# A four-stage image kernel: two PSUM banks for du*B with the products in front of the scans, transposes in one bank, and h in a ring of three

## The chip, the cores and the metric

One core of a Trainium2 chip. The metric is the device time of the kernel in microseconds, median over runs. The core has five engines that run their own in-order queues: TensorE (PE, matmuls, with weight loads shown as PEld), VectorE (DVE), ScalarE (ACT), GpSimd (POOL) and SyncE (SP, which issues most transfers). PSUM has eight banks of 128 partitions x 512 fp32 numbers.

## The reference

The input x is 32 images of 128 channels x 32 x 32, fp32. Four layers follow one another:

1. Quaternion batch normalisation. Channels form 32 groups of four; the covariance over batch and pixels is factored (Cholesky), and the input is whitened, mixed by a 4x4 weight per group and shifted. Once the statistics are known, this is one 128x128 matrix `m0` and a column of constants.
2. A Mamba block on each image as a sequence of L = 1024 pixels. With inner width 256 (two halves h of 128) and 16 states:

```
xn = layernorm(x);  xi, z = split(xn @ W_in.T)
xc = silu(causal_conv4(xi));  dt, B, C = split(xc @ W_x.T)
delta = softplus(dt @ W_dt.T + b_dt);  A = -exp(A_log)
h_t = h_{t-1} * exp(delta_t * A) + (delta_t * xc_t) * B_t      # 16 states for each inner channel
y_t = sum over states of h_t * C_t
out = ((y + xc * Dp) * silu(z)) @ W_out.T + x
```

3. Self-attention on the 1024 pixels of each image (one head, width 128), times gamma, plus its input.
4. A non-local block: again softmax attention on the 1024 pixels (theta, phi, a value projection), then batch normalisation over the whole batch, plus the input.

## The kernel before, in words

After the statistics of layer 1 (about the first 150 us) the kernel goes over the 32 images; the loops are unrolled, so every engine has its full list of instructions in a fixed order, and counting semaphores (`wait(engine, name, image, count)`) tie the lists together. The main function of each engine is `image(b, scan, more, att, late)`: while image b is in the scan, the attention stages of image b-1 and the tail of image b-2 run beside it, and the front part (layer norm to delta) of the next half image too. A batch normalisation over the stored results ends the kernel.

An image has two half images (chunks c = 0, 1 of 512 pixels) of 16 steps r = 0 to 15 each. A step k = 16 c + r serves one half h of the inner channels (r < 8 or r >= 8) and two of the 16 states (j = 0, 1). What a step does:

- ACT, `decay`: da = exp(delta * A) for the next step, two instructions (line 680), into a ring of two.
- DVE, `scans(b, k, j)`: `psD` = B row x du (line 484; du lies in PSUM as `psU`, copied there at r = 0 and r = 8, line 477) and the recurrence as one `tensor_tensor_scan` from da and psD into `hs` (line 488). For j = 0 and then j = 1. psD is one bank, so a product waits for the scan before it. hs is a ring of two (`sl = k % 2`).
- POOL, `products`: C rows x hs for both states (line 300), their sum (306), on odd steps the sum of two steps (310), and at r = 14, 15 delta and du for the next half image (286, 291).
- PE, `sum_states` ("add" in the order below): on odd steps adds POOL's result into psY by an identity matmul.
- DVE, `gate`: y * silu(z) from psY.

Attention works on 16 tiles of 128 queries for each image, eight for each half image, at steps `TILE_AT` = 7, 8, 10, 11, 13, 14, 16, 17 (16 and 17 are r = 0 and 1 of the next half image). Tile t goes: PE `energy` (1024 columns into the two banks of psE) -> DVE `row_max`, nm, at the end of the step (line 513) -> ACT `numer`, p = exp(E - max) (line 726) -> PE `turn`, eight transposes of p at steps `TURN_AT` = 8, 10, 12, 12, 14, 15, 17, 18, four into each bank of psT (line 987), -> ACT `turned_out`, two copies of psT into pt (line 690) -> PE `values` ("weigh0", "weigh1"), p times values for two tiles into psA -> ACT `spread`, rb (line 736) -> DVE `attended` (lines 528, 531, 535, 538). Energies of the next tile wait for p of this one, since psE is one pair of banks. `project` makes queries (psE) and keys (psT), `project_values` the values (psT).

The front part uses the same banks: centre, variance, inner0, gates and steps write psT, inner1 and rows psA. ACT reads them in `front(fb, fc, r)` at the steps AT_C = 0 and 1, AT_X = 5 and 7, AT_Z = 9, AT_B = 10, AT_P = 11 (and softplus's Exp and Ln at 13 and 14); it loads a table of functions for Silu and one to go back.

PSUM before: psE 2 banks, psT 2, psY, psU, psD, psA one each: all eight. PE's work within a step is a written list, `ORDER`. ACT's order within a step: key, front (r = 5), decay of the next step, spread, query, value, front (others), residual, turned_out, front (r = 9), numer.

## Time and profile before

| what | value |
| --- | --- |
| runs | 5652.95, 5642.84, 5648.49 us; median 5648.49 |
| profiled execution | 5654.98 us, its span 5653.2 us |
| mean granted TensorE clock | 0.955 |
| busy: PE | 4649.7 us (82%) |
| busy: DVE | 5067.2 us (90%) |
| busy: ACT | 3709.2 us (66%) |
| busy: POOL | 4724.3 us (84%) |
| DMA | 1216.87 MB, 215 GB/s |

The busy times are sums over the whole span; the statistics in front and the batch normalisation at the end use PE, DVE and POOL little, so the shares in the middle are higher. "PE busy" counts matmuls whose ends are modelled. A timeline row gives an instruction's start and duration, and neighbours on one engine can overlap by some hundredths of a microsecond; start-to-start distances are what adds up. Matmuls of fp32 are recorded as two instructions each.

### The profile page before, as it was taken

How to read it: one execution, taken by the hardware profiler on the slowest of the kernel's cores; microseconds unless marked ns; L12 is line 12 of the kernel's file. 1: busy time of each engine (PE TensorE's matmuls, PEld its weight loads, DVE VectorE, ACT ScalarE, POOL GpSimd, SP SyncE). 2: the span in 40 equal slices, each digit the busy share in tenths (PEclk: the TensorE clock that was granted, in tenths of full speed). 3: DMA queues.
4: the chain of work that ended last, by engine and by line, in shares of the span. 5: the costliest groups of instructions: out<-in, count | busy, mean ns of one | idle time of the engine just before them, and what ended most of it. 6: DMA issues, size and time to landing. Idle time of an engine off the chain costs nothing.

```text
span 5653.2 us, 61917 instructions
## 1 busy us (share of the span) xinstructions
PE 4649.7 (82%) x17331; PEld 2705.2 (48%) x17331; DVE 5067.2 (90%) x5978; ACT 3709.2 (66%) x6077; POOL 4724.3 (84%) x3342
## 2 busy tenths in 40 slices
PE   6568888888888888888888888888888888888871
PEld 6135554455445444545444455445445544554450
DVE  4699999999999999999999999999999999999933
ACT  3456677667766766676677667766666776677633
POOL 0698999999989889898989998989889899999910
PEclk9689999999999999999999999999999999999995
DMA  4456656655655565555556665665566566656517
GB/s 132 176 224 224 224 208 223 229 222 216 224 224 215 215 225 217 216 219 225 223 207 224 224 225 217 222 220 212 219 224 223 210 221 229 224 208 224 219 74 301
DMA packets 199100, 1216.87 MB, mean 215 GB/s; under 512 B 27881, under 2 KB 28657, under 8 KB 67697
## 3 DMA queue, kind: packets, MB, share of 16 engines
q1 hardware_dynamic: 194416, 1196.26, 57.4%
q10 hardware_dynamic: 4352, 16.78, 0.7%
q8 instruction: 136, 2.23, 0.2%
q14 instruction: 196, 1.60, 0.1%
HBM read 1158.43 MB, written 54.53 MB: 215 GB/s over the span
## 4 chain that ended last, share of the span: by engine, by line
PE 38%; DVE 22%; ACT 14%; issue 13%; POOL 10%; DMA 1%; DVEq 0%; SPq 0%; POOLq 0%; ACTq 0%
PE psA L814 13%; PE psE L814 11%; DVE hs L488 8%; DVE psD L484 7%; PE psT L814 7%; POOL pa L300 5%; PE psT L987 4%; ACT da L680 4%; ACT p L726 3%; DVE nm L513 3%; PE psY L814 2%; POOL pa L306 2%; POOL pa L310 1%; ACT L649 1%; ACT pt L690 1%
## 5 line engine op out<-in xcount | busy, mean ns | idle before, releaser
L300 POOL TENSOR_TENSOR pa<-hs,rows_all 128x1024 f32<-128x1024 f32 x1024 | 2412.8, 2356 | 396.8 <-DVE hs L488 396.5
L680 ACT ACTIVATE da<-delta,neg_a 128x512 f32<-128x512 f32 x2048 | 1382.1, 719 | 288.3 <-DVE hs L488 276.2
L484 DVE TENSOR_TENSOR psD<-rows_all,psU 128x512 f32<-128x512 f32 x2048 | 1416.5, 692 | 84.7 <-POOL hlast L304 6.3
L306 POOL TENSOR_TENSOR pa<-pa 128x512 f32<-128x512 f32 x1024 | 1317.1, 1286 | 40.2
L488 DVE TENSOR_TENSOR_SCAN hs<-da,hlast,psD 128x512 f32<-128x512 f32 x1024 | 1310.9, 1280 | 36.3
L488 DVE TENSOR_TENSOR_SCAN hs<-da,psD 128x512 f32<-128x512 f32 x1024 | 1249.4, 1220 | 35.2
L814 PE MATMUL psA<-pt,va 128*128 128x256 f32 x4096 | 989.5, 391 | 71.2 <-DVE x L531 43.7
L814 PEld LDWEIGHTS psA<-pt,va 128*128 128x128 f32 x4096 | 770.0, 194 | 295.5 <-DVE x L531 77.1
L513 DVE TENSOR_REDUCE nm<-psE 128x1 f32<-128x1024 f32 x512 | 620.1, 1211 | 201.1 <-PE psE L814 198.8
L726 ACT ACTIVATE p<-psE,nm 128x1024 f32<-128x1024 f32 x512 | 571.5, 1116 | 316.8 <-DVE nm L513 316.7
L690 ACT ACTIVATE pt<-psT 128x512 f32<-128x512 f32 x1024 | 555.5, 596 | 304.4 <-PE psT L987 301.0
L310 POOL TENSOR_TENSOR pa<-pa 128x512 f32<-128x512 f32 x512 | 651.1, 1272 | 40.1
L814 PE MATMUL psY<-pa,ident 128*128 128x512 f32 x1024 | 547.3, 617 | 156.0 <-POOL pa L310 153.5
L987 PE MATMUL psT<-ident,p 128*128 128x128 f32 x4096 | 546.6, 277 | 128.6 <-ACT p L726 128.6
L814 PE MATMUL psE<-ka,x 128*128 128x512 f32 x1024 | 530.8, 644 | 122.2 <-ACT p L726 122.2
L987 PEld LDWEIGHTS psT<-ident,p 128*128 128x128 f32 x4096 | 472.4, 143 | 317.3 <-issue 167.5
L814 PE MATMUL psE<-ka,qa 128*128 128x512 f32 x1024 | 505.5, 617 | 71.4 <-ACT p L726 71.4
L814 PEld LDWEIGHTS psE<-ka,x 128*128 128x128 f32 x1024 | 196.8, 201 | 371.9 <-issue 188.7
L814 PEld LDWEIGHTS psE<-ka,qa 128*128 128x128 f32 x1024 | 194.1, 195 | 330.1 <-issue 195.1
L814 PEld LDWEIGHTS psY<-pa,ident 128*128 128x128 f32 x1024 | 178.8, 194 | 350.8 <-issue 225.9
L286 POOL TENSOR_TENSOR delta<-delta,sp_l 128x512 f32<-128x512 f32 x128 | 163.1, 1274 | 179.8 <-ACT sp_l L671 179.8
L814 PE MATMUL psT<-xn,w_conv 128*128 128x512 f32 x512 | 235.2, 602 | 4.6 <-DVE xn L468 4.5
(186 smaller groups left out, 5017.6 us busy)
## 6 DMA issues: line engine op xcount, KB each, us to landing
rows_all<-bc_scratch SPq DMA_DIRECT2D x1024, 1024.0 KB, 4.7
xin<-x SPq DMA_DIRECT2D x40, 512.0 KB, 7.7
xres<-x SPq DMA_DIRECT2D x64, 256.0 KB, 6.1
x_scratch<-x SPq DMA_DIRECT2D x32, 512.0 KB, 4.3
f_scratch<-fa SPq DMA_DIRECT2D x32, 512.0 KB, 6.8
xres<-x SPq DMA_DIRECT2D x8, 512.0 KB, 3.6
x1g<-x SPq DMA_DIRECT2D x8, 512.0 KB, 3.7
fa<-x SPq DMA_DIRECT2D x8, 512.0 KB, 3.7
```

The costliest lines, as they stand in the source:

```text
L286: pool.tensor_tensor(delta[:, h, cols(fc)], delta[:, h, cols(fc)], sp_l[:, h, :], ALU.add).then_inc(S["delta_ok"], 1)
L300: pool.tensor_tensor(pa[:, k % PROD, :, :], hs[:, sl, :, :], rows_all[:, slot, 2:4, :], ALU.mult).then_inc(S["prod"], 1)
L306: pool.tensor_tensor(pa[:, k % PROD, 0, :], pa[:, k % PROD, 0, :], pa[:, k % PROD, 1, :], ALU.add).then_inc(S["pair"], 1)
L310: pool.tensor_tensor(pa[:, k % PROD, 0, :], pa[:, (k - 1) % PROD, 0, :], pa[:, k % PROD, 0, :], ALU.add).then_inc(S["quad"], 1)
L484: dve.tensor_tensor(psD[:, :], rows_all[:, slot, j, :], psU[:, :], ALU.mult).then_inc(S["dbu_ok"], 1)
L488: dve.tensor_tensor_scan(hs[:, sl, j, :], da[:, sl, j, :], psD[:, :], hlast[:, h, n_:n_ + 1] if ch else 0.0, ALU.mult, ALU.add).then_inc(S ...
L513: dve.tensor_reduce(nm[:, i % 2:i % 2 + 1], flat(psE), AX, ALU.max, negate=True).then_inc(S["nm_ok"], 1)
L680: act.activation(da[:, k % 2, j, :], delta[:, h, cols(ch)], ACT.Exp, scale=neg_a[:, h, 2 * q + j:2 * q + j + 1]).then_inc(S["da_ok"], 1)
L690: act.activation(pt[:, i // GT % 2, 4 * q:4 * q + 4, 128 * (t % GT):128 * (t % GT) + 128], psT[:, q, :].rearrange("p (j i) -> p j i", j=4) ...
L726: act.activation(p[:, i % 2, :], flat(psE), ACT.Exp, bias=nm[:, i % 2:i % 2 + 1], accum_out=rsum[:, i % (2 * GT):i % (2 * GT) + 1]).then_i ...
L814: return pe.matmul(dst, lhsT, rhs, start=start, stop=stop)
L987: last = pe.transpose(psT[:, q, 128 * j:128 * j + 128], p[:, i % 2, (4 * q + j) * 128:(4 * q + j + 1) * 128], ident[:, :])
```

## The change

- `psD` gets two banks, one for each j. `psA` loses its own bank and becomes the second bank of psT (`psA = psT[:, 1, :]`). Statistics' leftovers in psA and psD move accordingly.
- DVE: `scans` is split in `inputs` (the psU copy, now between the two scans of the last step of the group before), `spread_inputs` (both products, in front) and `scan_state`. The layer-norm product of r = 3 stands between products and scans.
- `hs` is a ring of three, indexed over images; da stays a ring of two.
- Transposes of a tile all go through psT's first bank, in two halves `turn0`, `turn1` (for the second tile of r = 12: `more0`, `more1`), each half waiting for ACT's copy of the one before it.
- Keys go through psE: `project` is split in `project_queries` (r = 5) and `project_keys` (r = 6, waits for the queries' copy); ACT's `key` moves behind decay and query. inner1 goes before keys and values, and its copy on ACT is at r = 6 (before: 7), in front of decay.
- gates and steps are split by half: gates1 at r = 8, gates0 at r = 9; steps0 at r = 11, steps1 at r = 12, both steps through the first bank, ACT's Abs and Relu at r = 11 and 12. The variance goes to the first bank.
- `residual` is split: its input matmul (`residual_input`, "resx") stands between the halves of a transpose.

```diff
@@
-        psD = ps("psD", [128, CH])
+        psD = ps("psD", [128, 2, CH])
         psT = ps("psT", [128, 2, CH])
-        psA = ps("psA", [128, CH])
+        psA = psT[:, 1, :]
...
-        AT_C, AT_N, AT_X, AT_Z, AT_B, AT_P = 0, 3, (5, 7), 9, 10, 11
+        AT_C, AT_N, AT_X, AT_Z, AT_B, AT_P = 0, 3, (5, 6), 9, 10, 11
...
-                    sl, slot = k % 2, k % RING
+                    sl, slot = (b * STEPS + k) % HRING, k % RING
...
+                def inputs(b, k):
+                    ch, h = divmod(k // PAIRS, NH)
+                    wait(dve, "du_ok", b, k // PAIRS + 1)
+                    wait(dve, "dbu_ok", b, 2 * k)
+                    dve.tensor_copy(psU[:, :], du[:, h, cols(ch)]).then_inc(S["u_ok"], 1)
+
+                def spread_inputs(b, k):
+                    slot = k % RING
+                    if k % PAIRS == 0:
+                        wait(dve, "u_ok", b, k // PAIRS + 1)
+                    at(dve, f"rl{slot}", (b * (STEPS // RING) + k // RING + 1) * 16)
+                    for j in range(2):
+                        wait(dve, "h_ok", b, 2 * (k - 1) + j + 1)
+                        dve.tensor_tensor(psD[:, j, :], rows_all[:, slot, j, :], psU[:, :], ALU.mult
+                                          ).then_inc(S["dbu_ok"], 1)
+
+                def scan_state(b, k, j):
...
+                    sl = (b * STEPS + k) % HRING
                     if j == 0:
-                        at(dve, f"rl{slot}", (b * (STEPS // RING) + k // RING + 1) * 16)
-                        wait(dve, "prod", b, k - 1)
-                        wait(dve, "hlast_ok", b, min(k - 1, NS))
-                    wait(dve, "h_ok", b, 2 * k + j)
-                    dve.tensor_tensor(psD[:, :], rows_all[:, slot, j, :], psU[:, :], ALU.mult).then_inc(S["dbu_ok"], 1)
+                        wait(dve, "prod", b, k - HRING + 1)
+                        wait(dve, "hlast_ok", b, min(k - HRING + 1, NS))
                     wait(dve, "dbu_ok", b, 2 * k + j + 1)
                     wait(dve, "da_ok", b, 2 * k + j + 1)
                     n_ = 2 * q + j
-                    dve.tensor_tensor_scan(hs[:, sl, j, :], da[:, sl, j, :], psD[:, :],
+                    dve.tensor_tensor_scan(hs[:, sl, j, :], da[:, k % 2, j, :], psD[:, j, :],
                                            hlast[:, h, n_:n_ + 1] if ch else 0.0, ALU.mult, ALU.add
                                            ).then_inc(S["h_ok"], 1)
...
                             if scan:
-                                scans(b, k, 0)
+                                spread_inputs(b, k)
                             if front_of and r == AT_N:
                                 normed(*front_of)
+                            if scan:
+                                scan_state(b, k, 0)
+                            if scan and k % PAIRS == PAIRS - 1 and (k < STEPS - 1 or more):
+                                inputs(*((b, k + 1) if k < STEPS - 1 else (b + 1, 0)))
...
                             if scan:
-                                scans(b, k, 1)
+                                scan_state(b, k, 1)
...
-                def turn(a, m, t, front):
+                def turn(a, m, t, q, front):
                     i = TILES * m + t
-                    wait(pe, "p_ok", a, i + 1)
...
-                    for q in range(2):
-                        wait(pe, "pt_ok", a, 2 * (i - 1) + q + 1)
-                        for j in range(4):
-                            last = pe.transpose(psT[:, q, 128 * j:128 * j + 128],
-                                                p[:, i % 2, (4 * q + j) * 128:(4 * q + j + 1) * 128], ident[:, :])
-                        last.then_inc(S["turn"], 1)
+                    if q == 0:
+                        wait(pe, "p_ok", a, i + 1)
...
+                    wait(pe, "pt_ok", a, 2 * i + q)
+                    for j in range(4):
+                        last = pe.transpose(psT[:, 0, 128 * j:128 * j + 128],
+                                            p[:, i % 2, (4 * q + j) * 128:(4 * q + j + 1) * 128], ident[:, :])
+                    last.then_inc(S["turn"], 1)
...
+                def project_keys(a, m, scan):
                     if m == 0:
...
+                        wait(pe, "q_ok", a, 1)
                     else:
                         wait(pe, "out_ok", a, NG // 2)
+                        if scan:
+                            wait(pe, "x1g_ok", a + 1, 1)
+                    for c in range(NCH):
+                        last = mm(psE[:, c, :], (w_k_t, tp_t)[m][:, :], (x1, x2)[m][:, cols(c)])
+                    last.then_inc(S["k_mm"], 1)
...
                 ORDER = [
                     "centre add variance",
-                    "add energy turn weigh0",
-                    "weigh1 turn add residual",
+                    "add energy turn0 weigh0 turn1",
+                    "weigh1 turn0 resx turn1 residual",
                     "weigh0 weigh1 add",
                     "inner0 add",
-                    "project add",
-                    "project_values add inner1",
+                    "query inner1 add",
+                    "key values",
                     "energy add",
-                    "skip0 energy turn add",
-                    "gates add energy_next",
-                    "rows turn add",
-                    "add energy steps weigh0",
-                    "turn weigh1 turn_more skip1 add energy_next",
+                    "skip0 energy turn0 gates1 turn1",
+                    "gates0 add energy_next",
+                    "rows turn0 turn1",
+                    "add energy steps0 weigh0",
+                    "steps1 weigh1 turn0 skip1 turn1 more0 energy_next more1",
                     "add",
-                    "weigh0 energy turn add",
-                    "turn weigh1 add energy_next",
+                    "weigh0 energy turn0 turn1",
+                    "turn0 weigh1 turn1 add energy_next",
                 ]
```

## Rows read from the trace of the kernel before

**Rows 1.** Busy us of PE, PEld, DVE, ACT, POOL in 2000:3000; clock, DMA share, GB/s

```profile
2000.00:3000.00 1000.00, 858.47 (x3140) 493.11 (x3138) 943.89 (x1089) 693.81 (x1145) 902.38 (x638) 0.98 0.60 220
```

**Rows 2.** Waits, whole span: who, for whom: us, times, longest

```profile
POOL pa L300 <- DVE hs L488: 396.5, 480, 2.6
...
DVE nm L513 <- PE psE L814: 198.8, 149, 7.0
...
DVE psD L484 <- POOL hlast L304: 6.3, 5, 2.1
```

**Rows 3.** Timeline of DVE, plain steps: start us, duration us, instruction

```profile
2726.06 1.28 DVE L488 TENSOR_TENSOR_SCAN hs<-da,hlast,psD 128x512 f32<-128x512 f32 x1
2727.38 0.70 DVE L484 TENSOR_TENSOR psD<-rows_all,psU 128x512 f32<-128x512 f32 x1
2728.11 1.28 DVE L488 TENSOR_TENSOR_SCAN hs<-da,hlast,psD 128x512 f32<-128x512 f32 x1
2729.53 0.70 DVE L484 TENSOR_TENSOR psD<-rows_all,psU 128x512 f32<-128x512 f32 x1
```

**Rows 4.** Timeline of DVE, scan before a row maximum

```profile
2701.32 1.28 DVE L488 TENSOR_TENSOR_SCAN hs<-da,hlast,psD 128x512 f32<-128x512 f32 x1
2702.51 1.20 DVE L513 TENSOR_REDUCE nm<-psE 128x1 f32<-128x1024 f32 x1
```

**Rows 5.** Timeline of DVE, gate before a product

```profile
2711.54 0.67 DVE L494 TENSOR_TENSOR du<-psY,sz 128x512 f32<-128x512 f32 x1
2712.13 0.69 DVE L484 TENSOR_TENSOR psD<-rows_all,psU 128x512 f32<-128x512 f32 x1
```

**Rows 6.** Page, part 5, transposes' copies: busy us, mean ns | idle before, releaser

```profile
L690 ACT ACTIVATE pt<-psT 128x512 f32<-128x512 f32 x1024 | 555.5, 596 | 304.4 <-PE psT L987 301.0
```

**Rows 7.** Timeline, row maxima of r = 7, 8, 11, 13, 14, 0 and what lies between

```profile
2737.69 1.20 DVE L513 TENSOR_REDUCE nm<-psE 128x1 f32<-128x1024 f32 x1
...
2743.50 1.20 DVE L513 TENSOR_REDUCE nm<-psE 128x1 f32<-128x1024 f32 x1
...
2744.73 1.11 ACT L726 ACTIVATE p<-psE,nm 128x1024 f32<-128x1024 f32 x1 [1.01 <-DVE nm L513]
...
2753.81 1.06 ACT L690 ACTIVATE pt<-psT 128x512 f32<-128x512 f32 x2
...
2759.70 1.23 DVE L513 TENSOR_REDUCE nm<-psE 128x1 f32<-128x1024 f32 x1 [1.25 <-PE psE L814]
...
2767.01 1.08 ACT L690 ACTIVATE pt<-psT 128x512 f32<-128x512 f32 x2 [0.55 <-PE psT L987]
...
2770.03 1.22 DVE L513 TENSOR_REDUCE nm<-psE 128x1 f32<-128x1024 f32 x1 [0.95 <-PE psE L814]
2770.14 0.63 ACT L671 ACTIVATE sp_l<-sp_e 128x512 f32<-128x512 f32 x1
...
2771.29 1.11 ACT L726 ACTIVATE p<-psE,nm 128x1024 f32<-128x1024 f32 x1 [0.51 <-DVE nm L513]
...
2775.92 1.20 DVE L513 TENSOR_REDUCE nm<-psE 128x1 f32<-128x1024 f32 x1
...
2785.56 1.20 DVE L513 TENSOR_REDUCE nm<-psE 128x1 f32<-128x1024 f32 x1
```

**Rows 8.** Chain of waits, r = 1 to 7 of another half image: start, us

```profile
2628.09 0.87 PE psT L987 x8
...
2640.21 0.86 PE psY L814 x2
...
2647.98 1.12 ACT ka L698
...
2654.64 1.73 PE psE L814 x4
```

**Rows 9.** Busy time by engine from p at r = 8 to p at r = 10

```profile
2744.73:2755.97 11.24, 7.64 (x23) 2.87 (x21) 10.89 (x13) 11.18 (x18) 9.64 (x6) 1.00 0.51 187
```

More of the change, by code:

```diff
@@ L381, in _ @@
                 dve.wait_ge(S["st_centred"], NB)
[L382 removed]
+                link(dve.tensor_copy(gram[:, :], psD[:, 0, 0:128]))
                 for j in range(4):
@@ L757, in image @@
                                 query(b - 1)
+                            if att and r == 6:
+                                key(b - 1, c)
                             if att and r == 7:
                                 value(b - 1, c)
-                            if front_of and r not in (AT_X[0], AT_Z):
+                            if front_of and r not in (*AT_X, AT_Z):
                                 front(*front_of, r)
@@ L846, in st_gram @@
                         blk = turned[q][:, 128 * j:128 * j + 128]
-                        last = mm(psD[:, 0:128], blk, blk, start=start and j == 0, stop=stop and j == 3)
+                        last = mm(psD[:, 0, 0:128], blk, blk, start=start and j == 0, stop=stop and j == 3)
                     last.then_inc(S["st_gram"], 1)
@@ L887, in front @@
                         mm(psT[:, 0, :], m0c[:, :], xin[:, cols(fc)]).then_inc(S["cent_mm"], 1)
-                    if what == "gates":
-                        if att:
-                            wait(pe, "pt_ok", *att["turned0"])
-                        else:
-                            wait(pe, "xi_ok", fb, 2 * fc + 2)
-                        for h in range(NH):
-                            mm(psT[:, h, :], w_in_t[:, DI + C * h:DI + C * h + C],
-                               xn[:, KC - 1 + fc * CH:KC - 1 + fc * CH + CH]).then_inc(S["z_mm"], 1)
@@ L896, in front @@
-                    if what == "steps":
-                        wait(pe, "rows_ok", fb, fc + 1)
-                        wait(pe, "z_ok", fb, 2 * fc + 2)
-                        if att:
-                            wait(pe, "pt_ok", *att["turned1"])
-                        for h in range(NH):
-                            mm(psT[:, h, :], w_dt_t[BCR:BCR + DR, C * h:C * h + C], rows_out[BCR:BCR + DR, :]
-                               ).then_inc(S["dpre_mm"], 1)
+                    if what in ("gates1", "gates0"):
+                        h = int(what == "gates1")
+                        wait(pe, "xi_ok", fb, 2 * fc + 2)
+                        if att and h == 1:
+                            wait(pe, "v_ok", *att["valued"])
+                        if att and h == 0:
+                            wait(pe, "pt_ok", *att["turned0"])
+                        mm(psT[:, h, :], w_in_t[:, DI + C * h:DI + C * h + C],
+                           xn[:, KC - 1 + fc * CH:KC - 1 + fc * CH + CH]).then_inc(S["z_mm"], 1)
@@ new lines, in front @@
+                    if what in ("steps0", "steps1"):
+                        h = int(what == "steps1")
+                        if h == 0:
+                            wait(pe, "rows_ok", fb, fc + 1)
+                            wait(pe, "z_ok", fb, 2 * fc + 2)
+                            if att:
+                                wait(pe, "pt_ok", *att["turned1"])
+                        else:
+                            wait(pe, "sp_abs", fb, 2 * fc + 1)
+                            wait(pe, "sp_relu", fb, 2 * fc + 1)
+                        mm(psT[:, 0, :], w_dt_t[BCR:BCR + DR, C * h:C * h + C], rows_out[BCR:BCR + DR, :]
+                           ).then_inc(S["dpre_mm"], 1)
@@ L955, in residual, with energy @@
                     last.then_inc(S["x1_mm"], 1)
-                def energy(a, m, t, scan):
+                def energy(a, m, t):
                     i = TILES * m + t
@@ L962, in energy @@
                         wait(pe, "k_ok", a, m + 1)
-                        if m == 1 and scan:
-                            wait(pe, "x1g_ok", a + 1, 1)
                     wait(pe, "p_ok", a, i)
@@ L1088, in work @@
                                             skip_term(b, c, int(what == "skip1"))
+                                    elif what == "resx":
+                                        if att and c == 0:
+                                            residual_input(b - 1, 1, beside.get("tile7"))
+                                        if scan and c == 1:
+                                            residual_input(b, 0, beside.get("tile7"))
                                     elif what == "residual":
@@ L1108, in work @@
                                         for half in range(2):
+                                            if what == f"turn{half}":
+                                                for m, t in turned_at(o)[0:1]:
+                                                    turn(a, m, t, half, front_of)
+                                            if what == f"more{half}":
+                                                for m, t in turned_at(o)[1:]:
+                                                    turn(a, m, t, half, front_of)
```

124 lines of the change are left out of this document (57 added, 67 removed).

## The prediction

> **What bounds the kernel now.** I read the busy shares of a steady stretch first [rows 1]: VectorE (DVE) is busy 94% of the time, GpSimd (POOL) 90%, TensorE (PE) 86%, ScalarE (ACT) 69%. Four engines in a fixed order are this close together, so I read the waits next [rows 2]: DVE waits in the scan stage for one thing, the energy tile that its row maximum `nm` reads (199 us in 149 waits, whole run), and POOL waits for DVE's scans (396 us). DVE is the pace-maker, with a few places where PE or ACT paces it. The timelines and the chain of waits then show which places.
>
> Names: a half image has 16 steps, r = 0 to 15; each holds two `psD` products and two scans. The 64 half images cover nearly all of the span. Softmax tiles have their energies, row maximum (nm) and exponential (p) at r = 0, 1, 7, 8, 10, 11, 13, 14, and the transposes of tile t follow one or two steps later.
>
> **The gain: DVE's junctions.** Starts in [rows 3] give product to dependent scan 0.73 us, scan to the product that must wait for its bank 1.32, and the last scan to the next step's product 1.42 (0.73+1.32+0.73+1.42 = 4.20 a step). Where the next instruction does not need the last, the same scan is followed after 1.19 [rows 4], and a DVE product of the same size by the next product after 0.59 for a duration of 0.67 [rows 5]. So a dependence costs 0.12 to 0.13 us a junction, 0.22 at a step's end. With two psD banks and both products in front, every neighbour is independent: 0.61+0.61+1.20+1.20 = 3.62 us a step. Per half image: 32 products x 0.12 = 3.8; the first scan in 11 steps (the other 5 already have work behind it) 1.3; the second scan in the 6 steps with no row maximum or attended part, x 0.22 = 1.3; the psU copy, now between scans, 0.2. Sum 6.6 us of 81.4. If all of it reached the end: 62 x 6.6 = 409 us. The junction product-product, both into PSUM, has no row; I bound its gain by 0 and 0.13 and take 0.12, since product after gate is the same kind.
>
> A rule speaks against it. The Trainium skill, page VectorE: DVE Perf Modes, section The DRAIN you can't avoid, says that a following Vector instruction cannot start until the pipe empties and that chaining without semaphores saves nothing (8 copies took the same time either way). By it the gain is 0; by the rows it is 6.6 us a half image. The trace disagrees with the rule here: 1.19 against 1.32 for the same scan.
>
> **The ring of three and `prod`.** DVE's waits for POOL are few (6.3 us for hlast) [rows 2]: a gain of 0 to 6 us over the run, taken as 0. Loads of rows_all still wait for the product four steps back, so they allow no longer lead than before; no product waits for a load now, taken as 0.
>
> **The cost: transposes in one bank.** A tile's 8 transposes went to two banks; ACT's two copies ran together, 1.06 us for the pair [rows 6, 7]. Now PE must wait for the first copy before the second four, and ACT for these. Four transposes take 0.43 us (0.87 for 8 in the chain, [rows 8]), a copy 0.60 [rows 6]; with hand-over both ways about 0.3, ACT's pair takes 0.60+0.43+0.60+0.3 = 1.9 instead of 1.06 even if PE answers at once, and longer where other matmuls stand between the halves (0.86 us for one of 512 columns, [rows 8]; 1.72 for half a weighing, its four matmuls having twice those columns in sum). ACT is in order, and behind the copies stand the exponential p and the next step's da; PE is in order too. An added wait can't gain; hidden, it costs 0. I now go from row maximum to row maximum.
>
> - **r = 7 to 8**, 5.81 us [rows 7], DVE-paced: nm 1.12, step 3.62, and the copy moved ahead: 4.8. -1.0.
> - **r = 8 to 11**, 16.20 us [rows 7]. From p (2744.73) ACT is busy 11.18 of 11.24 us [rows 9]: exp, da, table, silus, table, da, rows_out, two copies, exp. This is ACT's chain, and faster DVE steps don't shorten it. Nor can it start as early as nm allows: at r = 8 the second copy waits behind the gates matmul (0.43+0.86+0.43 us of PE after the energies), so p starts 2.0 after nm, not 1.23: +0.8. At r = 10 (`rows turn0 turn1`) the pair costs +0.85. In half images where this chain is shorter, DVE paces today, and the lengthened chain takes over. +1.5.
> - **r = 11 to 13**, 10.33 us, PE-paced [rows 7]: steps, weigh0, weigh1, transposes of two tiles, skip, energies. Same work, 1.15 us of ACT's Abs and Relu moved off, but the second pair must wait for a copy. +0.4.
> - **r = 13 to 14**, 5.89 us. Before, ACT has its last pair of copies done at 2768.1 and da, rb, exp and ln at 2770.8, before nm is done at 2771.25, so p starts at 2771.29 [rows 7]. Now `more1` comes after the energies: its copy ends 1.1 after nm could start; then the same da, rb, exp and ln, 2.8 in all (2770.77-2768.0), so p starts 3.9 after nm instead of 1.26. The attended part waits for rb, and with it weigh0 and the next energies (1.7 each). 7.1. +1.2.
> - **r = 14 to 0**, 9.64 us: DVE would need 9.1, PE 9.15 (transposes, weigh1, add, energies). -0.5.
> - **r = 0 to 1**: about 5.7 of 5.9 (DVE: nm, attended, one step of 4.0; then 3.6); PE and ACT's centre, variance, energies pace it. -0.2.
> - **r = 1 to 7**: in half images with a query projection PE paces from the transposes (2628.09) to the energies' end (2654.64+1.73): 28.3 us [rows 8]. Keys in psE remove the wait for the key copy (1.12 us), but the 0.86 us add that lay in it is bare again, and the r = 2 pair stalls PE 0.65: +0.3. In the others DVE paces and saves 1.8, of which 0.75 goes to a wait for p(7), held up by `turn1` behind weigh0: -1.1. Mean -0.4.
>
> Sum: -1.0+1.5+0.4+1.2-0.5-0.2-0.4 = +1.0 us a half image, x 62 (all but the first image's) = +62 us. The profiled execution took 5655.0 us (span 5653.2); that gives 5717, and as the median lies 6.5 lower, **5710 us**. DVE would then be nearer 87% busy and waiting.
>
> **Rivals.**
> (a) *The hand-overs hide.* ACT has 31% of slack, PE 14% [rows 1]; if ACT is at the copy each time and nothing urgent stands behind, only the fixed chains cap the gain: -1.0 (7 to 8), -0.4, 0, -0.3, -0.5, -0.2, and -1.1 for 1 to 7 = -3.5 us, x 62 = -217: 5432 us. For it: the size of the DVE saving, over six times the net that I forecast. Against: ACT has no gap exactly where a pair is lengthened [rows 9].
> (b) *POOL becomes the bound.* All of POOL's 396 us of waiting vanish [rows 2]: 5655-396 = 5259. It needs PE's 28 and 10 us chains shorter as well; nothing shortens them.
> (c) *Partial:* half of the hand-overs hide, -0.3 to -1.5 us a half image: 5555 to 5630.
> (d) *They cancel* within 0.2% (11 us, about what a measurement of this kernel can tell from no change).
> (e) *The junctions don't shorten,* since something in a product into PSUM or in its semaphore wait holds the next one back (the one junction without a row). Then the DVE-paced stretches give nothing (0 in place of -1.0, -0.5 and -0.2), r = 8 to 11 loses 0.7 since the late p hides behind the slower step, and 0.4, 1.2, 0.3 stay: +2.6 us, x 62: about 5810. It turns to my forecast's side only through the hand-overs, whose price is the same. Against: rows 4 and 5. The rule of the Trainium skill named above would make this case.
> The point that decides between forecast and (a) is the pairs at r = 8, 10 and 12: together above 3.5 us of delay it is slower.
>
> **How the numbers follow.** Forecast 0.44 (its own range +0.2 to +2.0 us a half image: 5660 to 5775), (a) 0.27, (b) 0.04, (c) 0.07, (d) 0.08, (e) 0.10. Faster 0.38, same 0.08, slower 0.54. The range, 5445 to 5810, reaches from most of (a) to (e) and leaves out (b) and the faster end of (a).
>
> **What would show it.** Right: psD to psD starts 0.6 apart and scan to scan 1.2; nm waiting for psE well above 199 us, mainly at r = 11, 13 and 14; ACT's pt waiting for PE above its 301 us [rows 6], the copies no longer in pairs; POOL's wait not smaller; 8 to 11 at 16 us or more, 13 to 14 near 7. Wrong: 13 to 14 still under 6 us, or 8 to 11 shorter (then (a)); or products still 0.7 apart (then (e)).

## The result and the profile after

The change makes the kernel slower: 5776.84 us median (5763.95 to 5781.74, six runs) against 5653.01, a ratio of 1.022 (95% interval 1.0207 to 1.0234), +124 us. I had forecast slower, at +62: the sign held, the forecast size was half of what came.

First the same steady stretch as [rows 1], in the same columns (us, then busy PE, PEld, DVE, ACT, POOL, clock, DMA, GB/s):

```profile
2000.00:3000.00 1000.00, 844.96 (x3094) 479.59 (x3092) 863.76 (x1064) 677.96 (x1118) 883.47 (x624) 0.98 0.58 215
```

DVE falls from 94% busy to 86%, and no other engine rises. What it waits for is in the list of waits of the kernel after (who, for whom: us, times, longest), which answers to [rows 2]:

```profile
ACT pt L704 <- PE psT L1006: 903.9, 808, 4.1
...
DVE nm L522 <- PE psE L828: 621.8, 326, 7.0
...
POOL pa L301 <- DVE hs L497: 397.4, 311, 2.7
...
PEld psT L1006 <- ACT pt L704: 331.8, 320, 1.9
...
PE psT L1006 <- ACT pt L704: 217.7, 260, 1.6
...
DVE rinv L513 <- ACT p L740: 67.5, 69, 3.8
...
DVE fa L544 <- ACT rb L750: 55.8, 36, 6.5
...
DVE psT L537 <- ACT rb L750: 48.7, 34, 4.7
```

The wait of nm for energies has grown from 199 to 622 us. ACT now waits 904 us for transposes (301 before, [rows 6]), in 808 waits for 1024 copies where there were 266 waits, and PE's transposes wait for ACT's copies (332 and 218 us), for which the list before has no row. POOL's wait stays at 397.

The DVE steps did become short. The timeline of DVE (start us, duration us), two steps with nothing else in them:

```profile
2603.99 1.28 DVE L484 TENSOR_TENSOR psD<-rows_all,psU 128x512 f32<-128x512 f32 x2
2605.18 2.44 DVE L497 TENSOR_TENSOR_SCAN hs<-da,hlast,psD 128x512 f32<-128x512 f32 x2
2607.54 1.27 DVE L484 TENSOR_TENSOR psD<-rows_all,psU 128x512 f32<-128x512 f32 x2
2608.72 2.44 DVE L497 TENSOR_TENSOR_SCAN hs<-da,hlast,psD 128x512 f32<-128x512 f32 x2
2611.08 1.26 DVE L484 TENSOR_TENSOR psD<-rows_all,psU 128x512 f32<-128x512 f32 x2
```

Two products take 1.18 us and two scans 2.36, start to start (0.59 and 1.18 for one), so a step is 3.54 us where [rows 3] had 4.20.

To find where the time went I take the starts of the eight row maxima of a half image and average the distances over seven half images (those between 2400 and 3060 us of each trace); the last column has the change over sixty half images of each trace. Times in us:

| from nm at r to nm at r | before | forecast change | after | change | change, sixty half images |
| --- | --- | --- | --- | --- | --- |
| 7 to 8 | 5.75 | -1.0 | 4.63 | -1.12 | -1.15 |
| 8 to 11 | 15.24 | +1.5 | 16.32 | +1.08 | +1.20 |
| 11 to 13 | 10.32 | +0.4 | 11.30 | +0.98 | +1.00 |
| 13 to 14 | 5.89 | +1.2 | 7.86 | +1.97 | +1.95 |
| 14 to 0 | 9.71 | -0.5 | 9.77 | +0.06 | -0.23 |
| 0 to 1 | 5.88 | -0.2 | 5.98 | +0.10 | +0.06 |
| 1 to 7 | 28.63 | -0.4 | 27.58 | -1.05 | -1.08 |
| sum | 81.42 | +1.0 | 83.43 | +2.0 | +1.74 |

1.74 us x 62 half images is 108 us, and the two profiled executions lie 109 us apart (5763.95 and 5654.98; the one after was the fastest of its six). That the seven half images' 2.0 us x 62 makes the 124 us between the medians is partly chance. The rows of one half image of the kernel after, in the order of [rows 7] (r = 7, 8, 11, 13, 14, 0, 1, 7):

```profile
2615.22 1.20 DVE L522 TENSOR_REDUCE nm<-psE 128x1 f32<-128x1024 f32 x1
...
2619.89 1.20 DVE L522 TENSOR_REDUCE nm<-psE 128x1 f32<-128x1024 f32 x1
...
2636.15 1.22 DVE L522 TENSOR_REDUCE nm<-psE 128x1 f32<-128x1024 f32 x1 [2.64 <-PE psE L828]
...
2647.45 1.23 DVE L522 TENSOR_REDUCE nm<-psE 128x1 f32<-128x1024 f32 x1 [2.93 <-PE psE L828]
...
2654.41 1.20 DVE L522 TENSOR_REDUCE nm<-psE 128x1 f32<-128x1024 f32 x1
...
2665.15 1.23 DVE L522 TENSOR_REDUCE nm<-psE 128x1 f32<-128x1024 f32 x1 [1.91 <-PE psE L828]
...
2671.13 1.22 DVE L522 TENSOR_REDUCE nm<-psE 128x1 f32<-128x1024 f32 x1 [0.53 <-PE psE L828]
...
2699.29 1.22 DVE L522 TENSOR_REDUCE nm<-psE 128x1 f32<-128x1024 f32 x1 [1.67 <-PE psE L828]
```

And ACT between r = 8 and 13, where the two copies of a tile ran as a pair before:

```profile
2620.16 0.60 ACT L704 ACTIVATE pt<-psT 128x512 f32<-128x512 f32 x1 [1.29 <-PE psT L1006]
2621.51 0.60 ACT L704 ACTIVATE pt<-psT 128x512 f32<-128x512 f32 x1 [0.75 <-PE psT L1006]
2622.00 1.11 ACT L740 ACTIVATE p<-psE,nm 128x1024 f32<-128x1024 f32 x1
...
2631.06 0.58 ACT L704 ACTIVATE pt<-psT 128x512 f32<-128x512 f32 x1
2632.38 0.60 ACT L704 ACTIVATE pt<-psT 128x512 f32<-128x512 f32 x1 [0.75 <-PE psT L1006]
2632.88 1.11 ACT L740 ACTIVATE p<-psE,nm 128x1024 f32<-128x1024 f32 x1
...
2647.89 0.60 ACT L704 ACTIVATE pt<-psT 128x512 f32<-128x512 f32 x1 [1.56 <-PE psT L1006]
2648.38 1.32 ACT L694 ACTIVATE da<-delta,neg_a 128x512 f32<-128x512 f32 x2
2649.61 0.37 ACT L750 ACTIVATE rb<-psT 128x256 f32<-128x256 f32 x1
```

The second copy starts 1.3 us after the first at best (ACT idle for 0.75 of them), where in a pair the starts were 0.48 to 0.5 apart: a hand-over (PE waits for a copy, ACT for the next transposes) costs ACT 0.85 us. At r = 8, p starts 2.1 after nm; at r = 13 the last copy (2647.89) comes after nm could start (2647.45), and da, rb and softplus behind it.

### The profile page after: what moved, and what is told of

Its sections match the earlier page's. It is cut to its first block, busy times and chain, and to the rows that moved or that the text cites. A ratio compares the mean times of both kernels' runs of the same rounds, so it can differ in the third digit from the quotient of the medians.

```text
span 5762.1 us, 62166 instructions
## 1 busy us (share of the span) xinstructions
PE 4653.2 (81%) x17331; PEld 2660.0 (46%) x17331; DVE 4746.2 (82%) x5978; ACT 3719.3 (65%) x6077; POOL 4722.2 (82%) x3342
## 4 chain that ended last, share of the span: by engine, by line
PE 55%; ACT 22%; DVE 10%; issue 9%; POOL 3%; DMA 1%; SPq 0%; DVEq 0%; ACTq 0%; POOLq 0%
PE psT L828 24%; PE psE L828 17%; PE psT L1006 8%; ACT da L694 6%; ACT p L740 6%; DVE hs L497 4%; PE psY L828 4%; ACT pt L704 3%; DVE nm L522 1%; ACT L663 1%; POOL pa L301 1%; ACT L763 1%; ACT sz L666 1%; DVE psD L484 1%; PE psD L828 1%
## 5 line engine op out<-in xcount | busy, mean ns | idle before, releaser
L301 POOL TENSOR_TENSOR pa<-hs,rows_all 128x1024 f32<-128x1024 f32 x1024 | 2412.3, 2356 | 397.4 <-DVE hs L497 397.4
L484 DVE TENSOR_TENSOR psD<-rows_all,psU 128x512 f32<-128x512 f32 x2048 | 1306.4, 683 | 4.4 <-DMA rows_all<-bc_scratch 4.2
L497 DVE TENSOR_TENSOR_SCAN hs<-da,hlast,psD 128x512 f32<-128x512 f32 x1024 | 1265.6, 1265 | 4.2 <-ACT da L694 4.2
L497 DVE TENSOR_TENSOR_SCAN hs<-da,psD 128x512 f32<-128x512 f32 x1024 | 1204.0, 1205 | 3.8 <-ACT da L694 3.8
L704 ACT ACTIVATE pt<-psT 128x512 f32<-128x512 f32 x1024 | 609.9, 596 | 907.1 <-PE psT L1006 903.9
L828 PE MATMUL psT<-pt,va 128*128 128x256 f32 x4096 | 1009.3, 393 | 133.9 <-DVE x L540 75.2
L828 PEld LDWEIGHTS psT<-pt,va 128*128 128x128 f32 x4096 | 767.4, 195 | 400.1 <-issue 125.0
L1006 PE MATMUL psT<-ident,p 128*128 128x128 f32 x4096 | 646.2, 281 | 331.8 <-ACT pt L704 217.7
L828 PE MATMUL psE<-ka,x 128*128 128x512 f32 x1024 | 496.0, 607 | 72.4 <-ACT p L740 72.3
L828 PE MATMUL psT<-xn,w_conv 128*128 128x512 f32 x1024 | 467.0, 600 | 3.5 <-DVE xn L469 3.5
L657 ACT ACTIVATE xc<-psT,cbias 128x512 f32<-128x512 f32 x128 | 87.9, 687 | 391.8 <-PE psT L828 391.8
```

The lines of the kernel that those rows point to most:

```text
L301: pool.tensor_tensor(pa[:, k % PROD, :, :], hs[:, sl, :, :], rows_all[:, slot, 2:4, :], ALU.mult).then_inc(S["prod"], 1)
L484: dve.tensor_tensor(psD[:, j, :], rows_all[:, slot, j, :], psU[:, :], ALU.mult).then_inc(S["dbu_ok"], 1)
L497: dve.tensor_tensor_scan(hs[:, sl, j, :], da[:, k % 2, j, :], psD[:, j, :], hlast[:, h, n_:n_ + 1] if ch else 0.0, ALU.mult, ALU.add).then ...
L704: act.activation(pt[:, i // GT % 2, 4 * q:4 * q + 4, 128 * (t % GT):128 * (t % GT) + 128], psT[:, 0, :].rearrange("p (j i) -> p j i", j=4) ...
L828: return pe.matmul(dst, lhsT, rhs, start=start, stop=stop)
L1006: last = pe.transpose(psT[:, 0, 128 * j:128 * j + 128], p[:, i % 2, (4 * q + j) * 128:(4 * q + j + 1) * 128], ident[:, :])
```

## The experiments

Each ratio is against runs of the kernel before made beside it on the same chip; the median of those runs lies between 5652.68 and 5662.58, so times of different experiments compare to within about 10 us. Theory T: the DVE half of the change gains, the hand-overs through one bank cost more. R1: the DVE half itself costs. R2: keys through psE and the new orders cost, not the bank (the expectation of run 4 has an R2 of its own). R3: 13 to 14 has another cause than the last copy. R4: another limit holds 14 to 0.

**1. The DVE half alone.**

```diff
-        psU = ps("psU", [128, CH])
-        psD = ps("psD", [128, CH])
+        psD = ps("psD", [128, 2, CH])
+        psU = psD[:, 1, :]
...
+                        dve.tensor_tensor(psD[:, j, :], rows_all[:, slot, j, :], psD[:, j, :], ALU.max
+                                          ).then_inc(S["dbu_ok"], 1)
```

> The kernel before with the DVE half of the change alone: two psD banks, both products in front of the scans, h in a ring of three; PE's and ACT's lists and the two banks for transposes stay as before. There are eight PSUM banks, so psU is left out: the product takes max(B row, psD) in place instead of B row x du, one input from PSUM and output to PSUM as before (the output isn't the reference's). Theory T (the DVE half gains, the hand-overs of transposes through one bank cost): DVE steps of 3.6 us in place of 4.2, capped by the PE and ACT chains that the prediction names (r = 8 to 11, 11 to 13), -3.5 us a half image: 5435 us (5400 to 5500). Rival R1 (the new order on DVE itself delays h for POOL or da for ACT, and that is the loss): 5653 or more. Rival of no overlap between two products into PSUM: products stay 0.7 us apart, 5580 or more.

Measured: 5453.18 us, ratio 0.963 (0.9611 to 0.9644). T, with its number 18 us low. R1 falls. 11 to 13 stays at 10.33 and 13 to 14 is 5.65: the chains of PE cap the gain as the prediction had them. The copies wait no more than before (277 us, 304 before), and nm waits more (the page's row of the copies, then the waits):

```profile
L706 ACT ACTIVATE pt<-psT 128x512 f32<-128x512 f32 x1024 | 555.8, 597 | 277.4 <-PE psT L1003 274.0
```

```profile
DVE nm L524 <- PE psE L830: 425.6, 243, 7.0
...
POOL pa L301 <- DVE hs L499: 202.0, 235, 2.7
```

A longer wait of nm is thus not in itself a loss: here DVE is fast and waits at PE's chains. POOL's wait is halved along with the gain.

**2. The PE and ACT half alone.**

```diff
-HRING = 3
+HRING = 2
...
-                                spread_inputs(b, k)
+                                scans(b, k, 0)
...
-                                scan_state(b, k, 1)
+                                scans(b, k, 1)
```

> The kernel after with its DVE half undone: products and scans one after the other through one psD bank and h in a ring of two, as before; transposes in one bank, keys through psE and the new orders on PE and ACT stay. Theory T: the stretches that DVE paces (r = 7 to 8 and 1 to 7) give back the 1.1 us each that they had gained, more where DVE is late at r = 14 and 0: 5777 + 62 x 2.2 to 3.5 = 5910 to 5990 us at most, not under 5800. Rival R1 (the DVE half is what costs): below 5777, towards 5653.

Measured: 5951.55 us, ratio 1.0517 (1.0498 to 1.0535). In the window of T. Alone, the halves are worth -209 and +289 us, +80 in sum; together they are +124. So the DVE half, worth 209 us alone, is worth 165 beside the other (289 less 124, each against its own runs of the kernel before).

**3. The ring of three alone.**

```diff
-        hs = sb("hs", [128, 2, 2, CH])
+        hs = sb("hs", [128, HRING, 2, CH])
...
-                        wait(dve, "prod", b, k - 1)
+                        wait(dve, "prod", b, k - HRING + 1)
```

> The kernel before with h in a ring of three and nothing else. Theory T: DVE waited 9 us in all for a free slot, so 5644 to 5656 us, no change. Rival (the ring lets DVE run ahead and move POOL's and PE's work): more than 10 us off on either side.

Measured: 5640.63 us, ratio 0.9969 (0.9955 to 0.9983): a small gain, against my "no change", and beyond the 10 us of the rival. It is small, but the runs of the two kernels don't overlap (5635 to 5654 us against 5658 to 5671). Of the distances only one moved much, 10 to 11, from 5.60 to 5.05; before, three of the seven half images took 6.3 to 6.4 there, and in such a one the energies ran at a mean granted clock of 0.54 (kernel before; columns as in the first fence):

```profile
2756.01:2759.70 3.69, 3.69 (x5) 1.28 (x6) 2.37 (x4) 1.18 (x2) 2.53 (x3) 0.54 0.71 276
```

In the run with the ring no half image of the stretch took over 5.3 there, but over the sixty half images of the whole trace 12 took 6.2 or more, against 18 before: the stretch shows the difference too large. Why a freer ring should spare PE the low clock isn't shown.

**4. Products in front without a second bank, written back to SBUF.**

```diff
-                    dve.tensor_tensor(psD[:, :], rows_all[:, slot, j, :], psU[:, :], ALU.mult).then_inc(S["dbu_ok"], 1)
+                        dve.tensor_tensor(rows_all[:, slot, j, :], rows_all[:, slot, j, :], psU[:, :], ALU.mult
+                                          ).then_inc(S["dbu_ok"], 1)
```

> The kernel before (two banks for transposes, psA of its own) with the products in front and the ring of three, without a second psD bank: B row x du is written back in place over the B row in SBUF, and the scan reads it there, so psD isn't used. Exact results. Theory T: if the scan (2.4 ns a column) isn't slowed by two inputs from SBUF, as e1: 5435 to 5500 us. Rival R2 (a DVE instruction with two SBUF inputs slows down while POOL works: the xn product took 0.6 or 1.66 us in the trace): scans of over 1.5 us, 64 a half image and in all 32 x 0.3 us or more, 5800 us and above.

Measured: 7151.69 us, ratio 1.2628 (1.2606 to 1.2649): the rival of this expectation. The page, part 5 (busy us, mean ns | idle before):

```profile
L301 POOL TENSOR_TENSOR pa<-hs,rows_all 128x1024 f32<-128x1024 f32 x1024 | 2690.5, 2627 | 459.0 <-DVE hs L496 459.0
L496 DVE TENSOR_TENSOR_SCAN hs<-da,hlast,rows_all 128x512 f32<-128x512 f32 x1024 | 2090.1, 2068 | 1.2 <-ACT da L693 1.2
L496 DVE TENSOR_TENSOR_SCAN hs<-da,rows_all 128x512 f32<-128x512 f32 x1024 | 1962.5, 1944 | 6.9 <-ACT da L693 5.7
L307 POOL TENSOR_TENSOR pa<-pa 128x512 f32<-128x512 f32 x1024 | 1753.7, 1713 | 40.1
```

A scan with both inputs in SBUF takes 1.94 to 2.07 us in place of 1.22 to 1.28, and POOL's instructions grow too (1713 ns from 1286, and 2627 from 2356), though a scan takes an element only each 2.4 ns (1.22 to 1.28 us for 512). A cause is named by the Trainium skill, in SBUF — State Buffer, section Who interferes with whom: a DVE instruction with two SBUF inputs contends with a GpSimd instruction that reads SBUF, as its second input comes through a read interface that both share. The trace agrees as far as durations go (some scans still take 1191 ns, others up to 3386). So with two SBUF inputs to each scan the DVE half loses far more than it gains, and of the ways tried a second bank is its price.

**5. A control for the left-out psU.**

```diff
-                        dve.tensor_tensor(psD[:, j, :], rows_all[:, slot, j, :], psU[:, :], ALU.mult
+                        dve.tensor_tensor(psD[:, j, :], rows_all[:, slot, j, :], psD[:, j, :], ALU.max
```

> A control: the kernel after with psU left out as in the run of the DVE half alone (max of B row and psD in place instead of B row x du; output isn't the reference's), everything else as after. Expected by every theory: as after, 5777 us, up to 10 more for the psU copy that now depends on the scan in front of it. If it is off by more than 15, the comparison with the DVE half alone has to be corrected by that.

Measured: 5757.59 us, ratio 1.0182 (1.0165 to 1.0199), 19 us under the kernel after (beside its own runs of the kernel before it stands at +105, the kernel after at +124). That is more than the 15 us that the expectation allowed, so the 209 us of run 1 are to be read as some 190; its sign stands. Run 6 is compared with this one.

**6. A bank for the second half of each tile's transposes.**

```diff
-                    wait(pe, "pt_ok", a, 2 * i + q)
+                    wait(pe, "pt_ok", a, 2 * (i - 1) + q + 1)
...
-                        last = pe.transpose(psT[:, 0, 128 * j:128 * j + 128],
+                        last = pe.transpose((psT[:, 0, :], psU[:, :])[q][:, 128 * j:128 * j + 128],
```

> The control with one thing changed: the bank that psU leaves goes to the second four transposes of each tile, so a half no longer waits for the copy of the half before it; orders, keys through psE and split gates and steps stay as after. Theory T (the hand-overs through one bank are the price): at r = 10 the pair shrinks from 1.9 to 1.1 us, at r = 12 the energies come 0.9 earlier; the matmuls that stand between the halves at r = 1, 8, 12 and 15 still hold ACT up. -2 to -3 us a half image: 5600 us (5570 to 5660). Rival R2 (keys through psE and the new orders cost, the bank doesn't): above 5720.

Measured: 5566.89 us, ratio 0.9848 (0.9831 to 0.9864), 191 us under its control from nothing but a second bank. That is T against R2, and a little under the lower end of T's window. At r = 10 the copies are a pair again; at r = 12 the second and third of four run together and the last stays alone (timeline of ACT):

```profile
2631.21 0.58 ACT L706 ACTIVATE pt<-psT 128x512 f32<-128x512 f32 x1
2631.69 0.58 ACT L706 ACTIVATE pt<-psU 128x512 f32<-128x512 f32 x1
...
2646.16 0.60 ACT L706 ACTIVATE pt<-psU 128x512 f32<-128x512 f32 x1 [1.51 <-PE psU L1008]
```

10 to 11 is 6.69 (7.54 in the control), 11 to 13 10.28 (11.30), 14 to 0 9.00 (9.35), 0 to 1 5.49 (5.98). 13 to 14 stays long, at 7.90 (7.63 over sixty half images, 7.81 in the control): the last copy behind the energies is a matter of order, not of the bank.

**7. At r = 12, both halves before the energies.**

```diff
-                    "steps1 weigh1 turn0 skip1 turn1 more0 energy_next more1",
+                    "steps1 weigh1 turn0 skip1 turn1 more0 more1 energy_next",
```

> The kernel after with one swap in PE's list at r = 12: both halves of the second tile before the energies of the next one (more0 more1 energy_next in place of more0 energy_next more1). Theory T: what lengthens r = 13 to 14 is the last copy behind the energies, which holds ACT's da, rb, softplus and p back. Now the copies end 1.7 us earlier and the energies 1.3 later: 11 to 13 12.3 us (11.3 after), 13 to 14 about 6.0 (7.9 after), sum -0.7 us a half image, 5735 us. Rival R3 (13 to 14 is long because of POOL or the attended part alone): 13 to 14 stays near 7.9, 5800 and more.

Measured: 5762.32 us, ratio 1.0193 (1.0176 to 1.021). 13 to 14 falls to 5.65 and 11 to 13 rises to 12.65: R3 is out. The time is 27 us above T's number: the gain of 0.9 in these two is half eaten by 14 to 0 (10.23), and more than half over sixty half images (-0.8 and +0.6).

**8. Tile 3 at r = 13.**

```diff
-        TURN_AT = [8, 10, 12, 12, 14, 15, 17, 18]
+        TURN_AT = [8, 10, 12, 13, 14, 15, 17, 18]
...
-                    "steps1 weigh1 turn0 skip1 turn1 more0 energy_next more1",
-                    "add",
+                    "steps1 weigh1 turn0 skip1 turn1 energy_next",
+                    "turn0 add turn1",
```

> The kernel after with the transposes of the second tile of r = 12 moved to r = 13, around its add: the energies no longer wait for a copy, and ACT has da, rb and softplus done before that tile's copies. Theory T: 11 to 13 falls to 10.4 us, 13 to 14 to about 6.3, -2.4 us a half image, 5620 to 5660 us: about as fast as before. Rival R3: under 1 us a half image, 5720 or more.

Measured: 5662.37 us, ratio 1.0017 (1.0008 to 1.0027), level with the kernel before and 2 us above T's window. 11 to 13 is 9.89 and 13 to 14 6.55, about as T says, but 14 to 0 rises from 9.8 to 10.9. Behind the pair of copies of tile 4 the exponential of tile 5, p(5), is late and PE idles; weigh1 behind it takes 3.15 us at a granted clock of 0.54 (1.73 where the clock stays full). The two stretches 14 to 0 and 0 to 1 of this kernel (columns as before, the clock third from last):

```profile
2612.07:2623.16 11.09, 8.62 (x35) 6.10 (x34) 8.85 (x11) 6.42 (x12) 10.78 (x8) 0.85 0.39 153
2623.16:2629.14 5.98, 4.53 (x12) 1.77 (x11) 5.41 (x7) 4.79 (x8) 3.99 (x4) 1.00 0.56 233
```

**9. Tile 4 at r = 15 too.**

```diff
-        TURN_AT = [8, 10, 12, 13, 14, 15, 17, 18]
+        TURN_AT = [8, 10, 12, 13, 15, 15, 17, 18]
...
-                    "weigh0 energy turn0 turn1",
-                    "turn0 weigh1 turn1 add energy_next",
+                    "weigh0 energy",
+                    "turn0 weigh1 turn1 add more0 energy_next more1",
```

> The kernel after with the second tile's transposes of r = 12 at r = 13 (as in the run before this) and, new, those of tile 4 moved from r = 14 to 15, in front of weigh1, and tile 5's around the energies there (turn0 weigh1 turn1 add more0 energy_next more1). In the run with tile 3 at r = 13, r = 14 to 0 took 10.9 us: the pair of tile 4 held p(5) back, PE stood idle and went into weigh1 at the low clock (0.85 mean over the stretch). Theory T: p(5) now starts right behind nm, PE has transposes and weigh1 to do in the meantime and keeps its clock: 14 to 0 9.1 us, -1.8 a half image: 5550 us (5520 to 5590), faster than the kernel before. Rival R4 (another limit, POOL or the centre stage, keeps 14 to 0 or 0 to 1 long): 5640 or more.

Measured: 5625.9 us, ratio 0.9938 (0.9922 to 0.9955). 14 to 0 is 8.77, better than expected, but 0 to 1 goes from 5.98 to 7.30: the centre matmul now waits for a last copy behind the energies (run 12 takes that copy away). The time lies between T's window and R4's: both in part.

**10. The hand-overs of r = 8 and 10.**

```diff
-                    "skip0 energy turn0 gates1 turn1",
+                    "turn0 energy turn1 skip0 gates1",
...
+                            if r == AT_B:
+                                for a, o in now:
+                                    turned_out(a, o, (0,))
```

> The same, with the two hand-overs on ACT's chain of r = 8 to 11 mended: at r = 8 turn0 energy turn1 skip0 gates1 (the gates matmul no longer stands between the halves), and at r = 10 ACT copies the first half in front of rows_out and the second behind it. Theory T: p(1) starts 0.8 earlier and the pair at r = 10 costs 0.5 less, 8 to 11 14.9 us (16.3 after), -1.3 a half image against the run above: about 5470 us. Rival (8 to 11 is not bound by ACT's chain): same time as the run above.

Measured: 5569.77 us, ratio 0.9841 (0.9824 to 0.9857). That is 56 us under run 9, where 80 were expected. 8 to 11 is 14.94 as expected (16.34 in run 9); 7 to 8 gives 0.55 back, where the energies now stand behind four transposes.

**11. A bank and the order of r = 12.**

```diff
-                    "steps1 weigh1 turn0 skip1 turn1 more0 energy_next more1",
+                    "steps1 weigh1 turn0 skip1 turn1 more0 more1 energy_next",
```

> The run with a bank of its own for each tile's second half (psU left out as there, the output isn't the reference's), and more0 more1 in front of energy_next at r = 12. What still divides that run (5567) from the one with the DVE half alone (5453) should be r = 13 to 14 (7.9 against 5.7 us), which theory T puts down to the last copy behind the energies. Expected by T: 13 to 14 5.7 us, 11 to 13 0.4 longer, -1.8 a half image: 5455 us, so that keys through psE and the split gates and steps cost nothing in sum. Rival R2 (those cost too): above 5520.

Measured: 5503.51 us, ratio 0.9725 (0.9708 to 0.9741), between the two bounds. 13 to 14 is 5.68 as said, but 11 to 13 costs 0.92 and not 0.4 more. Against the DVE half alone (5453) some 50 us stay: at 11 to 13 (11.20 against 10.33) and 8 to 11 (15.7 against 15.3 over sixty half images), part of which the new lists give back at 1 to 7 (27.52 against 28.02). Of the 0.9 at 11 to 13, 0.4 is the split of the steps (see below), and in the rest the second tile's last four transposes wait for a copy of the first tile even with a bank of their own, since the four halves now stand close together. So R2 is right for a small rest.

**12. Both halves of tile 5 before the energies.**

```diff
-                    "turn0 weigh1 turn1 add more0 energy_next more1",
+                    "turn0 weigh1 turn1 add more0 more1 energy_next",
```

> The last real version (8 to 11 mended) with one swap at r = 15: both halves of tile 5 in front of the energies (more0 more1 energy_next). There r = 14 to 0 is DVE's (8.8 us) and PE has over 2 us to spare, while r = 0 to 1 takes 7.0 us (6.0 in the kernel after), since the centre matmul waits for tile 5's last copy behind the energies. Theory T: 14 to 0 stays 8.8, 0 to 1 goes back to 6.0: -1.0 us a half image, 5508 us. Rival: the 1.2 us that the energies come later push 14 to 0 up by as much, no gain, 5560 to 5580.

Measured: 5544.7 us, ratio 0.9796 (0.9778 to 0.9813): 115 us under the kernel before and so nearly 240 under the kernel after, the best version. 0 to 1 is 5.98 as expected; 14 to 0 took 9.38, not 8.8, so of the 62 us expected under run 10 some 25 came, between T and its rival. Steady stretch:

```profile
2000.00:3000.00 1000.00, 875.78 (x3251) 497.48 (x3250) 908.27 (x1119) 708.75 (x1171) 924.09 (x650) 0.99 0.62 224
```

## Why the prediction was right in direction and half in size

The forecast of +62 us is the difference of two larger numbers: the DVE half at -217 (rival (a), all hand-overs hidden) and hence the rest at +279. Measured, the DVE half alone is -209 (some -190 by the control), and the rest on top of it +333 (some +315). The gain was right; the cost was short.

- **The gain at the junctions**: right. The step is 3.54 us (forecast 3.62), and alone the DVE half brings 209 us (some 190 by the control); the ring of three, which is part of it, brings 22 by itself. The junction without a row, product after product, takes 0.59, so rival (e) is out. (Its terms add up to +2.7 and not +2.6 us, which changes nothing.) By the rule that the prediction took from the Trainium skill (VectorE: DVE Perf Modes, The DRAIN you can't avoid) nothing could be gained; this kernel's trace has a scan followed after 1.18 to 1.19 us where it was 1.32. The same section adds that a next instruction that is not held starts earlier, which the prediction left out and which agrees with these starts.
- **The cost of one bank**: right in cause. A second bank and nothing else brings 191 us (run 6), so the hand-overs don't hide, and rival (a) is out.
- **7 to 8** right; **8 to 11** a little too dear (+1.5 for +1.08); **1 to 7** too dear (-0.4 for -1.05). Together I had 1.2 us too little gain. For 8 to 11 the closeness is in part luck: the 16.20 us that the prediction walked through come from one of the 18 half images in sixty whose energies at r = 11 ran at the low clock. The others took 14.5 to 15.1 before and take 16.3 to 16.4 after, and the low clock that no longer falls there gives some of it back.
- **The steps that failed** are the four from r = 11 to 1, which I had at +0.4, +1.2, -0.5 and -0.2, sum +0.9. They came to +0.98, +1.97, +0.06 and +0.10, sum +3.1 (over sixty half images +1.00, +1.95, -0.23 and +0.06, sum +2.8).

For **"r = 11 to 13 ... Same work"** the work was not the same. Before, the matmuls of the two steps stood together (timeline of PE in the kernel before):

```profile
2759.59 1.98 PE L814 MATMUL psT<-rows_out,w_dt_t 8*128 8x512 f32 x4
2761.50 1.99 PE L814 MATMUL psA<-pt,va 128*128 128x256 f32 x8
```

Steps0 and steps1 stand apart now. Timeline of PE in the kernel after:

```profile
2636.04 1.12 PE L828 MATMUL psT<-rows_out,w_dt_t 8*128 8x512 f32 x2
2637.09 1.99 PE L828 MATMUL psT<-pt,va 128*128 128x256 f32 x8
2639.02 1.12 PE L828 MATMUL psT<-rows_out,w_dt_t 8*128 8x512 f32 x2
2640.07 1.99 PE L828 MATMUL psT<-pt,va 128*128 128x256 f32 x8
...
2645.06 0.63 PE L1006 MATMUL psT<-ident,p 128*128 128x128 f32 x4 [0.78 <-ACT pt L704]
2645.53 1.88 PE L828 MATMUL psE<-ka,x 128*128 128x512 f32 x4
```

Start to start, the two steps' matmuls held PE for 1.91 us together and for 1.05 each apart; the weighing behind the first went from 1.83 to 1.93 and the second weighing from 1.73 to 1.83: 0.4 for the split. The transposes at 2645.06 start 1.42 us after the four in front of them, which take 0.44, because they wait for a copy: 1.0. Against that, the last four transposes (0.44) now stand behind the energies. 0.4 + 1.0 - 0.4 is the +0.98 of the table. Run 6, without the wait, took 10.28 (10.33 + 0.4 - 0.4), and run 8, with none of the second tile's transposes in front of the energies, 9.89. The prediction's +0.4 stood for the wait alone, which came to 1.0; it counted neither the split nor the transposes moved behind the energies.

For **13 to 14** the mechanism was right, and in the half images of the rows above (6.96 us; forecast 7.1) the size too. Every other half image is of another kind: there attended has two dependent parts, and PE stands idle behind it for 2.36 us and not 1.83. Six of these thirty took 7.4 us, and 24 took 9.0 to 9.1. What parts the six from the 24 is the clock: the granted clock over weigh0 (third from last) in one of the 24, in one of the other kind, and in one of the six:

```profile
2735.17:2738.09 2.92, 2.92 (x8) 2.37 (x9) 2.92 (x4) 2.92 (x6) 2.54 (x2) 0.62 0.00 0
2650.54:2652.37 1.83, 1.83 (x8) 1.51 (x9) 1.83 (x4) 1.83 (x4) 1.07 (x1) 1.00 0.29 116
570.01:571.84 1.83, 1.83 (x8) 1.62 (x9) 1.83 (x3) 1.83 (x5) 1.52 (x2) 1.00 0.00 0
```

The same eight records take 2.92 us between the two levels (1.2 and 2.4 GHz) and 1.83 at the full clock; the energies behind them take 2.32 in place of 1.72, at 0.74. Together that is the 1.7 us between 7.4 and 9.1. The sum had no such term. As the idle time before the weighing was 2.36 us in all thirty, it doesn't by itself decide the clock; what does isn't shown. Nor did the clock get lower as a whole: its mean over the run is 0.96 after and 0.955 before. The low stretches fall elsewhere: among others, in 18 of sixty half images at r = 10 to 11 before, in none there after, and in these 24 at r = 13 to 14 after.

For **14 to 0** I had let DVE or PE pace undisturbed and counted neither p(5)'s wait for tile 4's pair nor a low clock after it. In 52 of sixty half images it took 9.3 to 9.4 (forecast 9.14), and in eight 10.7 to 10.8, as in the stretch 2654.41 to 2665.15 of the rows above; PE is idle for 1.78 us in front of p(5)'s transposes in all of them. In run 8 the idle time is the same and 45 of sixty took 10.7 to 11.1; in run 9, with that pair out of the way, it is 8.77. For **0 to 1** a second bank brings 5.98 down to 5.5 (run 6), as in the DVE half alone (5.55), so the hand-overs are what ate the forecast gain of 0.2; at which place I haven't traced.

## What to carry to other kernels

Count what a freed PSUM bank was doing: two banks between PE and ACT are a queue of depth two, and with one the engines meet twice for each tile, here at 0.85 us of ACT's time and about 0.8 of PE's, in whatever stands behind them in order. When a bank must go, choose the places of the hand-overs by what is queued behind them. Runs 7 and 12 gained by ending a tile's copies before the next energies, so that no copy stands behind them; run 10 paid for energies behind four transposes with 0.55 us and gained more elsewhere. Here the places alone were worth nearly 240 us, more than the bank's 191. And walk the waits from one fixed point of a period to the next, over both kinds of half image, and give PE's clock a range of its own: it can move 1 to 2 us of a half image with no change in the order.

## What the runs showed of the hardware that I had not expected

- Two neighbouring DVE instructions that don't depend on one another start 0.09 to 0.1 us before the earlier one's recorded end (two products 1.18 us from 0.69 each; two scans 2.36 from 1.28 each), a dependent one 0.03 to 0.04 after it. The DVE half, which makes the neighbours independent and frees the ring, was worth 209 us of 5663 alone (some 190 by the control; 22 came with the ring by itself).
- A scan with two SBUF inputs slows down beside POOL: 1944 to 2068 ns on average in place of 1220 to 1280, and POOL's sum 1713 in place of 1286.
- Matmuls with 8 rows of contraction between matmuls of 128 cost 0.3 to 0.4 us more a visit than their columns (before, one visit of two: 1.91 and 1.83 us for 1.72 and 1.72; after, two visits of one: 1.05, 1.93, 1.05 and 1.83 for 0.86, 1.72, 0.86 and 1.72). Why isn't shown.
- The same PE list with the same idle time in front can run at either clock: after 2.36 us idle a weighing took 2.2 to 3.1 us in 24 half images and 1.83 in six.
- The ring of three by itself gained 0.3%, and I don't know how; whether it gains in the best version was not tried.
